# An attention kernel's L1 scores: the third of three halving adds taken off GpSimd, VectorE's last sum made twice as wide

## The reference

```
def one_query(qs):
    return -jnp.sum(jnp.abs(qs[:, None, :, :] - k), axis=-1) * scale
...
a = jnp.concatenate([a, jnp.zeros((b, 1, t, h), a.dtype)], axis=1)
a = jax.nn.softmax(a, axis=1)[:, :t]
```

## Time and profile before

| | |
|---|---|
| median of 3 runs | 3565.9 us (3556.08 to 3571.57) |
| the profiled execution | 3552.77 us, its span 3551.0 us |
| granted TensorE clock, mean | 0.987 of full speed |
| PE busy, weight loads busy | 3291.4 us (93%), 2433.9 us (69%) |
| DVE busy | 3124.4 us (88%) |
| POOL busy | 2845.6 us (80%) |
| ACT busy | 2691.1 us (76%) |

### The profile page before, as it was taken

One profiled execution on the slowest core, in us unless ns is written; L12 is line 12 of the kernel. 1 busy time (PEld: TensorE's weight loads), 2 busy tenths in 40 slices (PEclk: granted clock), 3 DMA queues, 4 the chain that ended last, 5 costly groups with the idle time before them and its releaser, 6 DMA issues. The chain is left out here.

```text
span 3551.0 us, 78815 instructions
## 1 busy us (share of the span) xinstructions
PE 3291.4 (93%) x23174; PEld 2433.9 (69%) x23174; DVE 3124.4 (88%) x4452; ACT 2691.1 (76%) x4796; POOL 2845.6 (80%) x2728
## 2 busy tenths in 40 slices
PE   8899999999999999999999999999999999999888
PEld 6676666766666776666776667766677666676655
DVE  6888989988999889988899988889898898888886
ACT  3777877777787777777777877777777777777774
POOL 3878888888888888887888888888888888888874
PEclk9999999999999999999999999999999999999999
DMA  6778778778787788777787877777777877777874
GB/s 140 157 152 161 152 152 159 153 153 162 154 159 151 154 158 159 156 150 144 154 164 152 162 147 155 157 156 155 155 153 154 163 151 157 151 154 152 164 156 86
DMA packets 198693, 543.75 MB, mean 153 GB/s; under 512 B 68054, under 2 KB 132438, under 8 KB 145656
## 3 DMA queue, kind: packets, MB, share of 16 engines
q0 software_dynamic: 73728, 501.78, 71.5%
q1 hardware_dynamic: 124920, 41.40, 6.1%
HBM read 10.79 MB, written 2.10 MB: 4 GB/s over the span
## 5 line engine op out<-in xcount | busy, mean ns | idle before, releaser
L918 DVE TENSOR_REDUCE S<-psU 128x16 f32<-128x1024 f32 x2182 | 2612.0, 1218 | 284.3 <-PE psU L481 276.1
L481 PE MATMUL psU<-flat,kT 99*128 99x256 bf16 x16384 | 2325.4, 276 | 223.0 <-ACT absd L706 104.4
L706 ACT ACTIVATE absd<-psU 128x1024 f32<-128x1024 f32 x1914 | 1953.0, 1024 | 626.8 <-PE psU L481 602.4
L481 PEld LDWEIGHTS psU<-flat,kT 99*128 99x128 bf16 x16384 | 1494.0, 98 | 911.3 <-DVE S L918 241.2
L1193 POOL TENSOR_TENSOR absd<-absd 128x1024 f32<-128x1024 f32 (+2 forms) x512 | 1173.6, 2292 | 204.3 <-DMA absd<-absd 203.1
L1182 POOL DMA_DIRECT2D absd<-absd x512 | 453.8, 886 | 296.3 <-ACT absd L706 250.2
L1197 POOL TENSOR_TENSOR absd<-absd 128x512 f32<-128x512 f32 (+2 forms) x512 | 609.5, 1190 | 40.2
L1200 POOL TENSOR_TENSOR absd<-absd 128x256 f32<-128x256 f32 (+2 forms) x512 | 351.5, 687 | 40.2
L493 PE MATMUL psC<-c1in,w 128*128 128x384 f32 (+1 forms) x930 | 312.1, 418 | 1.5 <-DVE c1in L962 0.8
L585 PE MATMUL psZ<-P,v 128*128 128x256 f32 x1024 | 309.0, 384 | 0.3 <-ACT P L824 0.3
L512 PE MATMUL psC<-c3in,w 128*128 128x128 f32 x1240 | 255.6, 290 | 5.2 <-DVE c3in L962 5.1
(11 more groups left out here) (178 smaller groups left out, 2212.7 us busy)
## 6 DMA issues: line engine op xcount, KB each, us to landing
absd<-absd POOLq DMA_DIRECT2D x413, 1024.0 KB, 7.9
flat<-qparts SPq DMA_DIRECT2D x3072, 8.0 KB, 4.0
absd<-absd POOLq DMA_DIRECT2D x64, 768.0 KB, 6.7
absd<-absd POOLq DMA_DIRECT2D x35, 512.0 KB, 4.8
xin<-in_x SPq DMA_DIRECT2D x32, 192.0 KB, 7.9
flat<-pattern SPq DMA_DIRECT2D x4, 768.0 KB, 10.7
out_h<-result SPq DMA_DIRECT2D x32, 64.0 KB, 5.9
w<-in_w SPq DMA_DIRECT2D x1, 1280.0 KB
```

The costliest lines, as they stand in the source:

```text
L481: mm = nc.tensor.matmul(psU[:, slot % PLACES, m], kT[0:ROWS + 3, b, m, :], flat[0:ROWS + 3, half % HALVES, :, lo:lo + BLOCK], start=True, ...
L706: nc.scalar.activation(absd[:, c % GROUPS, :, u], psU[:, slot % PLACES].rearrange("p (n a) s w -> p n (a s w)", n=2), ACT.Abs).then_inc(a_ ...
L918: nc.vector.tensor_reduce(S[:, b, hd, SB * c:SB * c + SB], psU[:, slot % PLACES].rearrange("p a s w -> p s a w"), AX.XY, ALU.add, apply_ab ...
```

## The change

GpSimd's third add for each group (8 numbers to 4) is left out, and VectorE's last sum reads 8 numbers of each 16 in place of 4. `LEVELS` and `WIDTH` follow. Nothing is placed at another slot.

```
-LEVELS = 3
-WIDTH = 4
+LEVELS = 2
+WIDTH = 8
...
                 lo, hi = rows[:, :, :, 0:8], rows[:, :, :, 8:16]
                 nc.gpsimd.tensor_tensor(lo, lo, hi, ALU.add).then_inc(a_tree, 1)
-                pool.wait_ge(a_tree, LEVELS * (TREES * i + c) + 2)
-                lo, hi = rows[:, :, :, 0:WIDTH], rows[:, :, :, WIDTH:2 * WIDTH]
-                nc.gpsimd.tensor_tensor(lo, lo, hi, ALU.add).then_inc(a_tree, 1)
```

## The result

| | before | after |
|---|---|---|
| median | 3561.1 us (3556.06 to 3571.57, 10 runs) | 3548.32 us (3545.89 to 3552.76, 10 runs) |
| the profiled execution | 3552.77 us, span 3551.0 | 3550.43 us, span 3548.6 |
| granted TensorE clock, mean | 0.987 | 0.988 |

The ratio is 0.9966, interval [0.9955, 0.9977]: 0.34% faster, 12.8 us between the medians. The forecast was 3593 us, 0.8% slower, with a range down to 3556. The prediction was wrong: the sign and the range both missed. It stood on three executions of before with a median of 3565.9 us; ten have 3561.1, and 5 us of the miss are that. The two profiled executions differ by 2 us only, since that of before is faster than all ten in the table and that of after is the third slowest of its ten. So the traces say where the waits lie, and the medians say what they cost.

A forecast was written before the change was run, and what follows sets the result against it. No single engine was taken to set the end: it passes round TensorE, VectorE and ScalarE. 0.40 x 98.5 us of VectorE's load less 12.4 us at L747 gave +27 us, 3593 us on the 3565.9 us median; range 3556 to 3650.

The forecast's parts named there:

- The price of the longer sum: VectorE's last sum L929: 1.05 ns per added element, 0.27 us per group of four heads, 128.6 us in all.
- The walk through the pair: Followed 16 groups of one image pair: L929's added time reaches TensorE in four, partly in the last, otherwise mostly swallowed by idle time.
- I take 0.40: Share of VectorE's net 98.5 us taken to reach the end, including an estimate for waits not yet in the trace.
- visible share: Part of VectorE's added time passing by waits the trace shows: 1.15 of 4.03 us a pair, 0.29, a lower end.
- 12.4 us of gain, all of it on the path: ScalarE's L747 waits 0.40 us less for GpSimd's root, 31 times, counted in full because TensorE waits there for ScalarE.
- VectorE's aggregate is late next: At L747, the wait shrinks by 0.40 us at most, not the add's 0.72, since the root then awaits VectorE's aggregate.
- GpSimd's own time isn't on the path, so I count only what waited for it: The removed third add was credited only with waits for GpSimd: L929's 30.1 us and 12.4 us at L747.
- L929's 30.1 us of waits: VectorE's last sum waited for GpSimd 55 times; these waits end, lowering VectorE's load from 128.6 to 98.5 us.
- Nothing else of GpSimd is waited for: Beyond L929 and L747, no wait for GpSimd counted; its transfer may issue earlier, awaited only on its own queue.
- GpSimd's lateness is what costs: Rival: L747's and L929's waits both vanish and a tenth of VectorE's load passes; -21 us, 3545 us, chance 0.10.
- VectorE as the bound: Rival: TensorE waits for VectorE behind nearly every group; 3682 us in full, 3623 us in part, chance 0.20 together.
- ring of engines: TensorE fills one of three PSUM places, VectorE or ScalarE empties it; the end passes from one engine to another.

The follow-up runs named there:

- e1: The change's GpSimd half alone on the kernel before: no third add, VectorE's last sum as short as before (half of each sum left out); 3514.17 us, 0.9877.
- e2: The change's VectorE half alone on the kernel before: all three GpSimd adds stay, VectorE's last sum reads 8 numbers; 3574.07 us, 1.0047.
- e8: The kernel before with ScalarE's step L747 at slot 8 in place of slot 6; 3552.91 us, 0.9975.
- e9: The kernel before, three adds, with VectorE's last sum (L929) at 19 slots in place of 17 and L747 at slot 8; 3560.16 us, 0.9985.
- e13: The kernel before with L929 at 19 slots, L747 at slot 8 and the third norm's root ahead of the three GpSimd adds; 3519.35 us, 0.9874.
- e6: The kernel before with VectorE's last sum (L929) 19 slots behind the group in place of 17; 3562.59 us, 0.9991.
- e14: The change with L747 at slot 8, and one slot more for ScalarE: the two-head group made one of three; 3573.69 us, 1.0028.
- e7: The changed kernel with ScalarE's step L747 at slot 8; 3536.86 us, 0.9921.
- e12: The change with L747 at slot 8, and four heads in all 16 groups, 64 ScalarE slots in place of 60; 3774.39 us, 1.0606.

## Why the prediction was wrong, point by point

**The price of the longer sum: right.** 0.27 us for a group of four was forecast (1.05 ns per element). The median instruction went from 409 ns to 674 ns. VectorE's busy time rose by 96.3 us only, to 3220.7 and not to some 3253; where the difference went wasn't traced.

**The walk through the pair: right in its visible part.** It named four places where the added time reaches TensorE. They are there in the trace of after, one pair of which runs from 979 us. These are its weight loads, and they answer to the earlier trace rows in this order: 1307.34 (0.44 us), 1312.81 (0.60), 1329.65 (0.20), 1367.44 (0.69), 1380.23 (0.55).

```profile
982.56 0.33 PEld L481 LDWEIGHTS psU<-flat,kT 99*128 99x128 bf16 x4 [0.56 <-DVE S L918]
...
988.25 0.11 PEld L613 LDWEIGHTS psZ<-ident,noh 128*32 128x32 f32 x2 [0.81 <-DVE qrest L1024]
...
1005.16 0.33 PEld L481 LDWEIGHTS psU<-flat,kT 99*128 99x128 bf16 x4 [0.46 <-DVE S L918]
...
1007.04 0.33 PEld L481 LDWEIGHTS psU<-flat,kT 99*128 99x128 bf16 x4
...
1042.61 0.77 PEld L481 LDWEIGHTS psU<-flat,kT 99*128 99x128 bf16 x8 [0.96 <-DVE S L918]
...
1055.67 0.33 PEld L481 LDWEIGHTS psU<-flat,kT 99*128 99x128 bf16 x4 [0.82 <-DVE S L918]
```

The waits grew by 0.12, 0.21, 0.26, 0.27 and 0.27 us. The third is the one that the walk called swallowed: the load at 1331.79 had waited 0.37 us for ScalarE, and its counterpart at 1007.04 has no wait left.

**"I take 0.40": too high.** Between e1 and the change only the sum's length differs: 36.2 us of 128.6, a share of 0.28. The walk's visible share was 0.29. The 0.11 that I added for passes that the trace doesn't show was not there. That made the cost 51 us in place of 36 (0.40 and 0.28 of 128.6). That 0.28 and 0.29 lie so close is in part luck: the walk was made in the trace with the third add in it, and there (e2) the longer sum cost 14 us, a share of 0.11.

**L747, "12.4 us of gain, all of it on the path": too high twice.** "VectorE's aggregate is late next" was the right sentence, but it left a smaller gain than 0.40 us a pair. The wait fell by 5.5 us in all, not by 12.4, and its place is taken by GpSimd's wait for that aggregate. And e8 passed only 0.41 of such a wait on. The timeline of after:

```profile
1031.53 0.25 DVE L948 BATCH_NORM_AGGREGATE mvn<-stn 128x2 f32<-128x6 f32 x2 [0.15 <-DVEq L946]
1031.85 0.19 POOL L1209 TENSOR_TENSOR ven<-mvn,small 128x2 f32<-128x2 f32 x1 [0.73 <-DVE mvn L948]
...
1033.51 0.77 ACT L747 ACTIVATE x<-h,nmrn,rstdn 128x64 f32<-128x64 f32 x2 [0.66 <-POOL nmrn L1218]
```

The wait in the earlier trace rows was 1.00 us, here it is 0.66: a third of a microsecond for a root that starts 0.73 us after GpSimd is free.

**"GpSimd's own time isn't on the path, so I count only what waited for it": the step that failed.** It gave the add 12.4 us by L747 and, with L929's 30.1 us of waits counted as if they were VectorE's work, 0.4 x 30.1 = 12 us by those, 24 in all. The add cost 46. L747's part of that is 2 to 5 us by the shares measured, so the mis-sized term is L929's. Two things were wrong with it. Its price: from e9 to e13 22.6 us of VectorE's named waits for GpSimd went, and 41 us with them, more than the whole and not 0.4 of it. And its place: at the third convolution GpSimd's add and root set VectorE's pace in nearly every pair, while the list names a wait of L929 there in 12. "Nothing else of GpSimd is waited for" was true of the list only; the root behind the add was waited for too. That masked wait doesn't add to the 46 us, but it is why L929's waits could be moved away (e6, e9) without any gain. With the shares as measured, -46 + 36 gives the -10 of that chip, near the result's -12.8.

**The rivals.** "GpSimd's lateness is what costs" is what happened in kind, with 3545 us against 3548.32. But that its number is near is luck: it took the 30.7 us of L747's wait as gone, of which 5.5 went, and a tenth of the longer sum as passing, of which 0.28 passed. What had cost the time was VectorE held by GpSimd, at the groups' sums and at the third convolution's root. I gave it 0.10 because I tested it at L747 alone. VectorE as the bound did not come: with 91% busy its longer sum passed a share of 0.28. The Trainium skill (Perfetto Trace Analysis, Identifying the Most-Contended Engine) would improve the fullest engine first. By itself, loading VectorE did cost here (e2 is 0.47% slower than before, and the change 36 us slower than e1). But the fullest engine wasn't where the time lay: the third add of GpSimd, 80% busy, cost more than that, e13 gained 41 us over e9 with the busy shares as they were, and relieving VectorE by one slot (e14) came out slower than e7.

**What would have shown it beforehand.** At 1520.31 to 1521.42 all rows stood in the trace of before: an engine that waits, and the next thing that it needs from the same engine, done only 0.12 us before it is used. The same 0.12 us in pair after pair says that the one is released by the other, though no wait is named.

## What to carry to other kernels

Where an engine waits for another, look at the next thing that it takes from the same engine, and ask when that would be ready if the first wait were gone; a wait of the list may cover one that the list lacks. Look also for pairs of instructions on two engines whose distance is always the same small number: there one engine holds the other, listed or not. An engine's step costs what stands behind it in its queue, so try to move the short, urgent step (a root of 0.9 us) ahead of the long ones (adds of 4.3 us) before taking work away: e13, with all three adds, is 29 us faster than the change, and 17.5 us faster than the change with L747 at slot 8 (e7). The change with the root moved too was not run. For the price of added work in a ring of engines, the places where the trace shows a wait (0.29) were a better estimate than the same with a supplement for unseen ones (0.40 against 0.28 measured), in this one case.

## What the runs showed of the hardware that I had not expected

**The granted clock fell after two short pauses of TensorE.** In the episode of before, TensorE stood 0.55 us and 0.64 us, at 1522 and 1523 us. The stretches around it (length, busy PE, PEld, DVE, ACT, POOL, granted clock, DMA share, GB/s):

```profile
1518.00:1522.00 4.00, 3.53 (x26) 2.60 (x24) 2.75 (x7) 3.54 (x6) 3.77 (x6) 1.00 0.89 173
1522.00:1524.00 2.00, 1.27 (x7) 0.94 (x8) 2.00 (x3) 0.00 (x0) 1.27 (x2) 0.85 0.70 138
1524.00:1527.00 3.00, 3.00 (x17) 2.34 (x17) 2.52 (x7) 1.71 (x2) 2.84 (x3) 0.53 1.10 221
1527.00:1530.00 3.00, 3.00 (x26) 2.49 (x23) 2.54 (x4) 1.96 (x4) 2.46 (x3) 1.00 0.52 101
```

From 1524 to 1527 us the clock is at 0.53, near its lower level of 1.2 GHz, while TensorE is shown busy without a gap, and afterwards at 1.00 again, 2.4 GHz. A pause alone doesn't foretell it: the timeline of e13 has a longer one, and its clock is at 1.00 from 1508 to 1520 us.

```profile
1508.83 0.61 PE L481 MATMUL psU<-flat,kT 99*128 99x256 bf16 x4 [0.94 <-DVE S L918]
...
1508.00:1512.00 4.00, 3.17 (x22) 2.23 (x23) 3.88 (x7) 3.54 (x6) 3.91 (x3) 1.00 1.03 208
1512.00:1516.00 4.00, 3.94 (x35) 3.25 (x33) 3.90 (x11) 2.96 (x5) 3.92 (x4) 1.00 0.67 128
```

What decides it isn't settled here.

**A pause of 2.82 us, and then some 20 us at half clock.** In e12, the kernel with 64 slots of ScalarE's, ScalarE stands once a pair without a wait that the trace names, 118.3 us over 28 times. Timeline and stretches of e12:

```profile
1318.65 1.02 ACT L706 ACTIVATE absd<-psU 128x1024 f32<-128x1024 f32 x1 [4.15 <-issue]
...
1319.73 4.55 PE L481 MATMUL psU<-flat,kT 99*128 99x256 bf16 x20 [2.82 <-ACT absd L706]
```

```profile
1320.00:1340.00 20.00, 20.00 (x90) 13.78 (x89) 15.18 (x25) 12.95 (x19) 12.74 (x14) 0.53 0.53 105
1340.00:1350.00 10.00, 10.00 (x70) 7.66 (x70) 8.79 (x10) 9.47 (x27) 5.85 (x5) 1.00 0.87 172
```

TensorE stands 2.82 us and then works some 20 us at a clock of 0.53, near its lower level of 1.2 GHz, without a gap, and only then is back at 1.00. e12's mean clock is 0.923 against 0.987 for before. It lies 238 us over e7; how much of that is the stalls and how much the clock was not taken apart. What holds ScalarE there is open: the trace has "issue" for it, and no run tried to take it away.
